# A routed feed-forward kernel on one core: 40 matmuls ahead of the first work, the token list made in one piece, tied gathers, and one transpose for the left-over columns of a routed pair

## The chip, the cores and the metric

One core of a Trainium2 chip runs the whole program. The metric is device time in microseconds (us) of one execution. Engines: PE is the matmul engine (PEld its weight loads), DVE the vector engine, ACT the scalar engine, POOL the general engine, SP the queue that only issues DMAs.

## The reference

4096 tokens (128 batches of 32) with 256 features go through two layers.

```python
# x: (128, 32, 256); subjects and adapters: one of 8 per batch
t = einsum('bct,bcd->bdt', x, w[subjects]) + b[subjects]       # 32x32 mix inside a batch
scores = softmax(t @ gate_w.T); top 2 of 8 experts             # routing
for e in range(8):                                             # routed part, inner size 176
    y += dense_w[:, e] * ((silu(t @ w1[e].T) * (t @ w3[e].T)) @ w2[e].T)
z = (silu(t @ sw1.T) * (t @ sw3.T)) @ sw2.T                    # shared part, inner size 352
x = x + y + z
H = x @ W.T + ((x @ A[adapter].T) @ B[adapter].T) * s          # second layer: linear with adapters
x = x + fp8dot(gelu(fp8dot(H, wg0)) * fp8dot(H, wg1), w_linear)  # hidden size 1024, fp8 operands
```

## The kernel before

The program is written by hand, one instruction stream for each engine, with semaphores between them. The order of the streams is the order of the code; no scheduler moves anything. Tokens are handled in 32 tiles of 128 (`TILES`), four to a group, so 8 groups of 512 tokens (`GROUPS`); `EARLY` is 6.

Products in full precision are made of three matmuls over high and low halves in fp32r (`three`, L1096, L1097 and L1098). ACT writes the high half of an operand (a copy that rounds) and DVE the low half (a subtraction).

The stages, with their time in the profiled execution:

1. **Opening, 0 to 44 us.** For each group: DVE picks the 32x32 matrices of the batches (L659, L660) and spreads them into block-diagonal operands `bd` (L671, semaphore `bd_ready`); PE multiplies (`condition`, L1110); ACT adds the bias (`conditioned`, L448); PE transposes (L1122); ACT keeps the transposed tile (`keep_xT`, L461); PE makes the router's logits (`router`, L1130). SP loads `x` and stores the result `kept`.
2. **Shared part and list, 44 to 128 us.** PE runs `shared_up` and `shared_down` of groups 0 to 5 while DVE sorts out the routing. The slots of the experts are filled by a sum of outer products: `listed` (L1170) multiplies 64 one-hot pairs into bank 5, and DVE turns the sum into the gather indices `perm` (L901). In the same stretch DVE writes the low halves of the routed weights of experts 2 to 7 (`routed_weight_lo`, L752), which `routed_up` waits for (`rw_split`).
3. **Routed part, 128 to 281 us.** 71 slot tiles in 36 pairs (`PAIRS`; the last holds one tile). For a pair POOL gathers the tokens (L387), and PE takes these steps: `routed_T` (transpose of the tokens, L1235), `routed_up` (L1096 to L1098, 352 columns), `routed_hT` (transpose of the hidden values, L1257), `routed_down` (back to 256 columns). The loop runs `routed_T(n + 1)`, `routed_hT(n - 1)`, `routed_up(n)`, `routed_down(n - 1)`. The inner size of 176 is 128 + 48, so a tile's hidden values `hr` are transposed in two blocks; DVE writes the 48 left-over columns twice (at 0 and at 64, L919), so that after the transpose partitions 0 to 47 can hold their high half and 64 to 111 their low half (L930).
4. **Shared part of groups 6 and 7, first gathers, 281 to 317 us.** POOL gathers the two expert results of each token from `slots_out` (`gather_tile`, L394, two DMAs a tile), DVE combines them (L975, L982), and PE starts the second layer for group 0 (`adapters_down`, `linear`, `adapters_up`). DVE clips its result to fp8 (`to_h8`, L1009, waits for `H_done`), which the first fp8 matmul waits for.
5. **Second layer, 317 to 458 us.** For each group `ffn_up` (L1346, 8 steps of 4 matmuls), `ffn_down` (L1365), and between them the next group's linear part. In each group POOL adds the residual of the previous one (`final`, L409) and gathers two groups ahead: `gather(g)` waits for `comb_done` alone, and then issues its 8 DMAs one after the other.

The last group is written out by halves of two tiles: `ffn_down(g, 0)` then `ffn_down(g, 1)`, each followed by a copy on ACT, an addition on DVE and a store on SP.

## Time and profile before

| | us |
|---|---|
| median of 3 runs | 458.88 |
| lowest and highest | 458.27, 459.74 |
| the profiled execution | 459.88 |
| its span, first to last instruction | 458.1 |
| mean granted clock of PE | 0.987 of full |

The span lies 1.78 us under the time of the same execution. "Idle before" of a row is the time in which the engine did nothing ahead of it, and what ended it. PEclk is the granted clock of PE as a share of 2.4 GHz.

### The profile page before, as it was taken

The numbers are of one execution on the slowest core, as the hardware profiler recorded it, in microseconds if no ns is written. First come the engines' busy times: TensorE is split into PE (matmuls) and PEld (weight loads), VectorE is DVE, ScalarE is ACT, GpSimd is POOL, SyncE is SP. The second block draws the span as 40 slices with busy tenths as digits, with TensorE's granted clock in tenths as the row PEclk, the third lists the DMA queues.
The fourth block names the chain that finished last, engine by engine and source line by source line (L and its number), as shares of the span: only waits on it lengthen the run. The fifth ranks groups of instructions, "written<-read, shape, count | busy, mean of one in ns | idle before, by whom it ended". The sixth has DMA issues, their size and how long they took to land.

```text
span 458.1 us, 8166 instructions
## 1 busy us (share of the span) xinstructions
PE 432.9 (95%) x2732; PEld 354.9 (77%) x2732; DVE 309.4 (68%) x701; ACT 249.2 (54%) x514; POOL 181.9 (40%) x188
## 2 busy tenths in 40 slices
PE   4899999999969999999999999995999999999996
PEld 3798788887769999999999997873567557557563
DVE  6972587899774666665666653663967867867844
ACT  2578445658314565555555553432754854855844
POOL 0000506930063444444444401675045756756120
PEclk9999999999998999999999999998899999999999
DMA  7988330000052555545555541332022332322111
GB/s 220 326 286 260 113 110 0 1 0 1 2 156 70 172 155 159 158 150 159 144 174 156 154 102 69 87 99 81 0 72 69 113 92 73 104 90 84 47 46 47
DMA packets 37383, 50.40 MB, mean 110 GB/s; under 512 B 4608, under 2 KB 30592, under 8 KB 37344
## 3 DMA queue, kind: packets, MB, share of 16 engines
q1 hardware_dynamic: 30000, 31.81, 21.1%
q0 software_dynamic: 6480, 17.70, 14.6%
q8 instruction: 24, 0.39, 0.3%
q10 hardware_dynamic: 864, 0.37, 0.3%
q14 instruction: 15, 0.12, 0.1%
HBM read 32.17 MB, written 17.69 MB: 109 GB/s over the span
## 4 chain that ended last, share of the span: by engine, by line
PE 86%; DVE 4%; ACT 3%; issue 2%; another core or an unknown queue 2%; DMA 1%; POOL 1%; SPq 0%; DVEq 0%
PE bank L1096 16%; PE bank L1097 15%; PE bank L1098 15%; PE bank L1346 13%; PE bank L1365 6%; PE bank L1110 4%; PE bank L1257 3%; PE bank L1235 3%; PE bank L1130 3%; PE bank L1273 2%; PE bank L1272 2%; PE bank L1312 2%; PE bank L1122 1%; PE bank L1170 1%
## 5 line engine op out<-in xcount | busy, mean ns | idle before, releaser
L387 POOL DMA_INDIRECT xg<-kept,perm x71 | 67.6, 952 | 102.6 <-PE bank L1235 61.1
L1346 PE MATMUL bank<-h,wg 128*128 128x512 fp8e4 x256 | 64.0, 393 | 4.8 <-DVE h L1009 4.8
L1346 PEld LDWEIGHTS bank<-h,wg 128*128 128x128 fp8e4 x256 | 23.1, 100 | 40.0 <-ACT ff L610 11.8
L928 DVE TENSOR_TENSOR hrl<-bank,hrh 128x256 fp32r<-128x256 f32 (+1 forms) x36 | 15.2, 422 | 54.2 <-ACT hrh L552 52.9
L1096 PE MATMUL bank<-w13h,xgl 128*128 x142 | 49.5, 348 | 0.0
L608 ACT ACTIVATE gel<-bank 128x512 bf16<-128x512 f32 x64 | 40.1, 627 | 12.2 <-PE bank L1346 9.1
L1098 PE MATMUL bank<-w13h,xgh 128*128 x142 | 46.5, 327 | 0.0
L1097 PE MATMUL bank<-w13l,xgh 128*128 x142 | 46.3, 326 | 0.0
L394 POOL DMA_INDIRECT ga<-slots_out,slot x32 | 31.8, 994 | 28.7 <-SPq L347 18.7
L610 ACT ACTIVATE ff<-bank 128x512 bf16<-128x512 f32 x64 | 40.6, 635 | 0.3 <-PE bank L1346 0.3
L394 POOL DMA_INDIRECT gb<-slots_out,slot x32 | 36.8, 1148 | 9.8 <-issue 9.8
L1096 PE MATMUL bank<-xsh,sw13l 128*118 128x512 f32 (+1 forms) x96 | 38.5, 401 | 1.5 <-ACT sil L490 0.8
L559 ACT ACTIVATE yr<-bank 128x512 f32<-128x512 f32 (+1 forms) x36 | 21.3, 592 | 33.9 <-PE bank L1273 33.9
L1021 DVE TENSOR_TENSOR actb<-gel,ff 128x512 bf16<-128x512 bf16 x64 | 27.6, 431 | 17.2 <-ACT ff L610 17.1
L409 POOL TENSOR_TENSOR fin<-xm,ob 128x512 f32<-128x512 f32 x14 | 16.2, 1155 | 55.6 <-ACT ob L616 52.1
L1098 PE MATMUL bank<-xsh,sw13h 128*118 128x512 f32 (+1 forms) x96 | 37.8, 394 | 0.0
L547 ACT ACTIVATE silr<-bank 128x176 f32<-128x176 f32 x71 | 22.8, 321 | 26.1 <-PE bank L1098 23.5
L1365 PE MATMUL bank<-wl,act 128*128 128x256 fp8e4 x256 | 33.1, 273 | 0.4 <-DVE act L1029 0.4
L1365 PEld LDWEIGHTS bank<-wl,act 128*128 128x128 fp8e4 x256 | 23.7, 98 | 10.3 <-issue 3.7
L377 POOL TENSOR_SCALAR places<-cst,placef 128x72 f16<-128x72 f32 x28 | 23.0, 841 | 19.9 <-DVE placef L811 19.9
L1097 PE MATMUL bank<-xtL,sw13h 128*118 128x512 f32 (+1 forms) x72 | 28.3, 393 | 0.0
L616 ACT ACTIVATE ob<-bank 128x512 bf16<-128x512 f32 x16 | 9.6, 597 | 33.6 <-PE bank L1365 33.6
(180 smaller groups left out, 1187.4 us busy)
## 6 DMA issues: line engine op xcount, KB each, us to landing
slots_out<-yr SPq DMA_DIRECT2D x35, 256.0 KB
xres<-in_x SPq DMA_DIRECT2D x7, 512.0 KB, 5.3
kept<-xtr SPq DMA_DIRECT2D x7, 512.0 KB, 3.2
out_x<-fin SPq DMA_DIRECT2D x7, 512.0 KB
w13raw<-in_rw SPq DMA_DIRECT2D x8, 352.0 KB, 3.5
w2raw<-in_rw SPq DMA_DIRECT2D x8, 256.0 KB, 3.7
wgst<-in_wgate SPq DMA_DIRECT2D x16, 128.0 KB
xg<-kept,perm POOLq DMA_INDIRECT x71
```

The source lines that it names most:

```text
L377: pool.tensor_scalar(places[:, c, :], cst[:, C_J:C_J + SLOT_TILES], placef[:, c:c + 1], cst[:, C_TOKEN + t:C_TOKEN + t + 1], ALU.is_equal, ...
L387: pool.indirect_dma_start(out=xg[:, i % 2, j, :], out_offset=None, in_=kept, in_offset=bass.IndirectOffsetOnAxis(perm[:, 2 * i + j:2 * i + ...
L394: pool.indirect_dma_start(out=buf[:, g % 2, j, :], out_offset=None, in_=slots_out, in_offset=bass.IndirectOffsetOnAxis(slot[:, k, g * GT + ...
L547: act.activation(silr[:, j, :], bank[j][:, 0:INNER], ACT.Silu).then_inc(s("silr_ready"), 1)
L608: act.activation(gel[:, b, :], bank[b][:, :], ACT.Gelu_apprx_tanh).then_inc(s("gel_ready"), 1)
L610: act.activation(ff1[:, b, :], bank[2 + b][:, :], ACT.Copy).then_inc(s("ff1_ready"), 1)
L1021: dve.tensor_tensor(actb[:, c % 4, :], gel[:, b, :], ff1[:, b, :], ALU.mult).then_inc(s("act_ready"), 1)
L1096: pe.matmul(dst, al, bh, start=first, stop=False, skip_group_check=True)
L1097: pe.matmul(dst, ah, bl, start=False, stop=False, skip_group_check=True)
L1098: return pe.matmul(dst, ah, bh, start=False, stop=last, skip_group_check=True)
L1346: ins = pe.matmul(bank[bk][:, :], wg8[:, kk, half, c * P:(c + 1) * P], h8[:, k, kk, :], start=(kk == 0), stop=(kk == KC - 1))
L1365: ins = pe.matmul(bank[6 + half][:, (j % 2) * D:(j % 2 + 1) * D], act8[:, c, j * P:(j + 1) * P], wl8[:, c, :], start=(c == 0 and j % 2 == ...
```

## The change

Seven edits are made at once:

- **Warm.** PE issues 40 matmuls of 128 columns on a constant (`onesb`) ahead of `condition(0)`; POOL writes that constant first. SP issues the load of the table ahead of that of the subjects.
- **`keep_xT(0)`** stands ahead of `conditioned(1)` on ACT.
- **List.** All 64 products of `listed` stand ahead of `shared_up(5)` parts 2 to 5, where 32 stood ahead of parts 2 and 3 and 32 behind them. On DVE `perm` stands two steps earlier, and `shared_x_lo(EARLY)` (L682) behind `routed_mul(0)`.
- **Gathers.** `gather(g)` waits ahead of tile j for `gate_done` of step 2j of `ffn(g - 2)`.
- **One transpose.** The left-over columns of both tiles of a pair lie in one block (`hr[:, 2]`, 48 at column 0, 48 at column 64), so that a pair has three transposes, the third into bank 7. ACT copies it with an instruction of its own, broadcast to both tiles; DVE then writes the low half of tile 0 at partitions 64 to 111 and that of tile 1 at 0 to 47, in two instructions. `hr_hi` and `hr_split` count two steps a pair, and `routed_down` waits for the second only ahead of its last four matmuls.
- **Last group.** Tiles 0 and 1 go through bank 6, tile 2 through bank 3, tile 3 through bank 4, each with its own copy, addition and store.

```diff
@@ sync
+            sp.dma_start(tabr[:, :, :].rearrange("p j e -> p (j e)"), table).then_inc(s("table_in"), 16)
             sp.dma_start(subj[:, :], subjects).then_inc(s("subj_in"), 16)
-            sp.dma_start(tabr[:, :, :].rearrange("p j e -> p (j e)"), table).then_inc(s("table_in"), 16)
...
@@ gpsimd
                 pool.wait_ge(s("comb_done"), (g - 1) * GT)
                 for j in range(GT):
+                    pool.wait_ge(s("gate_done"), (g - 2) * HC + 2 * j + 1)
                     gather_tile(g, j)
...
@@ scalar
             conditioned(0)
+            keep_xT(0)
             conditioned(1)
-            keep_xT(0)
...
-                act.activation(hrh[:, 0:n, :, :].rearrange("p a b c -> p (a b c)"), bank[4][:, 0:n * 2 * P], ACT.Copy).then_inc(s("hr_hi"), 1)
+                act.activation(hrh[:, 0:n, 0, :], bank[4][:, 0:n * P].rearrange("p (a b) -> p a b", a=n), ACT.Copy
+                               ).then_inc(s("hr_hi"), 1)
+                act.activation(hrh[:, 0:n, 1, :], bank[7][:, 0:P].unsqueeze(1).broadcast_to([P, n, P]), ACT.Copy
+                               ).then_inc(s("hr_hi"), 1)
...
@@ vector, routed_mul
-                    dve.tensor_tensor(hr[:, j, P:2 * P].rearrange("p (a b) -> p a b", a=2)[:, :, 0:REST],
-                                      silr[:, j, P:INNER].unsqueeze(1).broadcast_to([P, 2, REST]),
-                                      bank[j][:, INNER + P:2 * INNER].unsqueeze(1).broadcast_to([P, 2, REST]),
+                    dve.tensor_tensor(hr[:, 2, j * LO_AT:j * LO_AT + REST], silr[:, j, P:INNER], bank[j][:, INNER + P:2 * INNER],
                                       ALU.mult).then_inc(s("hr_ready"), 1)
...
@@ vector, routed_h_lo
-                dve.tensor_tensor(hrh[low, 0:n, 1, :], of_tile[low, :, 1, :], hrh[low, 0:n, 1, :].bitcast(F32),
-                                  ALU.subtract).then_inc(s("hr_split"), 1)
+                                  hrh[:, 0:n, 0, :].bitcast(F32), ALU.subtract).then_inc(s("hr_split"), 1)
+                dve.wait_ge(s("hr_hi"), 2 * i + 2)
+                spare = slice(LO_AT, LO_AT + REST)
+                for j, own, other in ((0, slice(0, REST), spare), (1, spare, slice(0, REST)))[0:n]:
+                    ins = dve.tensor_tensor(hrh[other, j, 1, :], bank[7][own, 0:P], hrh[own, j, 1, :].bitcast(F32), ALU.subtract)
+                ins.then_inc(s("hr_split"), 1)
...
@@ tensor
+            pe.wait_ge(s("c_prep"), 1)
+            for _ in range(WARM):
+                pe.matmul(bank[3][:, 0:P], onesb[:, :], onesb[:, :], start=True, stop=True)
             condition(0)
...
-            listed(0, ENTRIES // 2)
-            shared_up(EARLY - 1, parts=range(2, 4))
-            listed(ENTRIES // 2, ENTRIES)
-            shared_up(EARLY - 1, parts=range(4, 6))
+            listed()
+            shared_up(EARLY - 1, parts=range(2, 6))
...
                 for j in range(tiles_of(i)):
-                    for c in range(2):
-                        col = (j * 2 + c) * P
-                        ins = pe.transpose(bank[4][:, col:col + P], hr[:, j, c * P:(c + 1) * P], ident)
+                    pe.transpose(bank[4][:, j * P:(j + 1) * P], hr[:, j, :], ident)
+                ins = pe.transpose(bank[7][:, 0:P], hr[:, 2, :], ident)
...
+            def last_down():
+
+                g = GROUPS - 1
+                pe.wait_ge(s("ob_ready"), g * 2)
+                for c in range(HC):
+                    pe.wait_ge(s("act8_ready"), g * HC + c + 1)
+                    for j in range(2):
+                        ins = pe.matmul(bank[6][:, j * D:(j + 1) * D], act8[:, c, j * P:(j + 1) * P], wl8[:, c, :],
+                                        start=(c == 0 and j == 0), stop=(c == HC - 1), skip_group_check=True)
+                ins.then_inc(s("down_done"), 1)
+                for j, _, b in LAST[1:]:
+                    for c in range(HC):
+                        ins = pe.matmul(bank[b][:, 0:D], act8[:, c, j * P:(j + 1) * P], wl8[:, c, :],
+                                        start=(c == 0), stop=(c == HC - 1))
+                    ins.then_inc(s("down_done"), 1)
```

How the instructions move, at three places.

DVE, from the low halves of expert 3's weights to the first routed product. Before:

```order
L752 TENSOR_TENSOR w13l<-w13raw,w13h 128x704 [waits rw_hi]
L752 TENSOR_TENSOR w2l<-w2raw,w2h 128x512
L901 TENSOR_SCALAR perm<-bank 128x72 [waits r_listed]
L733 TENSOR_TENSOR hsf<-sil,bank 116x512 [waits hs_split,u_done,sil_ready]
L752 TENSOR_TENSOR w13l<-w13raw,w13h 128x704 [waits rw_hi]
L752 TENSOR_TENSOR w2l<-w2raw,w2h 128x512
L740 TENSOR_TENSOR hsl<-hsf,hsh 116x512 [waits hh_ready]
L752 TENSOR_TENSOR w13l<-w13raw,w13h 128x704 [waits rw_hi]
L752 TENSOR_TENSOR w2l<-w2raw,w2h 128x512
L682 TENSOR_TENSOR xsh<-xtT,xsh 128x1024 [waits u_done,xs_hi]
L912 TENSOR_TENSOR xgl<-bank,xgh 128x512 [waits xr_hi,hs_split]
L912 TENSOR_TENSOR xgl<-bank,xgh 128x512 [waits xr_hi]
```

And with the change:

```order
L769 TENSOR_TENSOR w13l<-w13raw,w13h 128x704 [waits rw_hi]
L769 TENSOR_TENSOR w2l<-w2raw,w2h 128x512
L914 TENSOR_SCALAR perm<-bank 128x72 [waits r_listed]
L750 TENSOR_TENSOR hsf<-sil,bank 118x512 [waits hs_split,u_done,sil_ready]
L769 TENSOR_TENSOR w13l<-w13raw,w13h 128x704 [waits rw_hi]
L769 TENSOR_TENSOR w2l<-w2raw,w2h 128x512
L757 TENSOR_TENSOR hsl<-hsf,hsh 118x512 [waits hh_ready]
L769 TENSOR_TENSOR w13l<-w13raw,w13h 128x704 [waits rw_hi]
L769 TENSOR_TENSOR w2l<-w2raw,w2h 128x512
L750 TENSOR_TENSOR hsf<-sil,bank 116x512 [waits hs_split,u_done,sil_ready]
L769 TENSOR_TENSOR w13l<-w13raw,w13h 128x704 [waits rw_hi]
L769 TENSOR_TENSOR w2l<-w2raw,w2h 128x512
```

The row that makes `perm` stood behind the third weight pair of this stretch and now stands behind the first; the pieces of hidden values and weights that stood ahead of it now come behind it.

PE, the step between two pairs of the routed loop (tokens' transposes, hidden values' transposes, first product of the next pair). Before:

```order
L1235 MATMUL bank<-cst,xg 128x128 [waits xr_split,xg_in1]
L1235 MATMUL bank<-cst,xg 128x128 x3
L1257 MATMUL bank<-cst,hr 128x128 [waits hr_split,hr_ready]
L1257 MATMUL bank<-cst,hr 128x128 x3
L1096 ISA [waits hr_ready,xr_split]
L1096 MATMUL bank<-w13h,xgl 128x352
```

And with the change:

```order
L1249 MATMUL bank<-cst,xg 128x128 [waits xr_split,xg_in1]
L1249 MATMUL bank<-cst,xg 128x128 x3
L1269 MATMUL bank<-cst,hr 128x128 [waits hr_split,hr_ready]
L1269 MATMUL bank<-cst,hr 128x128
L1270 MATMUL bank<-cst,hr 128x128
L1110 ISA [waits hr_ready,xr_split]
L1110 MATMUL bank<-w13h,xgl 128x352
```

Four transposes of `hr` have become three, and the third has a line of its own.

DVE, the low halves of one routed pair and the next pair's first steps. Before:

```order
L928 TENSOR_TENSOR hrl<-bank,hrh 128x256 [waits hr_hi]
L930 TENSOR_TENSOR hrh<-bank,hrh 48x2x128
L912 TENSOR_TENSOR xgl<-bank,xgh 128x512 [waits xr_hi]
L918 TENSOR_TENSOR hr<-silr,bank 128x128 [waits silr_ready]
L919 TENSOR_TENSOR hr<-silr,bank 128x2x48
```

And with the change, where `hrh` is written by two instructions of 128 columns, behind a wait of their own, for one of 256:

```order
L941 TENSOR_TENSOR hrl<-bank,hrh 128x256 [waits hr_hi]
L946 TENSOR_TENSOR hrh<-bank,hrh 48x128 [waits hr_hi]
L946 TENSOR_TENSOR hrh<-bank,hrh 48x128
L928 TENSOR_TENSOR xgl<-bank,xgh 128x512 [waits xr_hi]
L934 TENSOR_TENSOR hr<-silr,bank 128x128 [waits silr_ready]
L935 TENSOR_TENSOR hr<-silr,bank 128x48
```

The low half of the left-over columns has gone from one row to two, and the products of these columns (`hr`, 48 columns) are half as wide.

## Rows read from the trace of the kernel before

**Rows 1.** The page: busy time, share of the span and instructions by engine.

```profile
PE 432.9 (95%) x2732; PEld 354.9 (77%) x2732; DVE 309.4 (68%) x701; ACT 249.2 (54%) x514; POOL 181.9 (40%) x188
```

**Rows 2.** Window of the routed loop: length, busy by engine, PEclk, DMA share, GB/s.

```profile
138.00:272.00 134.00, 133.81 (x990) 132.65 (x991) 81.75 (x268) 73.80 (x169) 59.13 (x63) 0.99 0.52 148
```

**Rows 3.** The chain, 0 to 60 us: start, us, what.

```profile
1.18 2.81 DMA tabr<-in_table
...
5.97 2.07 PE bank L1110 x4
...
12.23 1.96 PE bank L1110 x8
...
15.05 0.98 ACT xtT L461 x2
...
20.80 1.73 PE bank L1110 x8
```

**Rows 4.** Timeline of DVE, 0 to 46 us: start, us, line, operation [idle before].

```profile
10.22 0.69 DVE L671 TENSOR_TENSOR bd<-wrow,cst 128x512 f32<-128x512 f32 x1
...
16.59 0.69 DVE L671 TENSOR_TENSOR bd<-wrow,cst 128x512 f32<-128x512 f32 x1
```

**Rows 5.** The chain, 100 to 146 us.

```profile
115.72 2.58 PE bank L1170 x32
...
129.88 2.55 DMA xg<-kept,perm
...
134.78 2.53 another core or an unknown queue
```

**Rows 6.** Timeline of PE, 100 to 146 us.

```profile
130.31 0.63 PE L1235 MATMUL bank<-cst,xg 128*128 128x128 f32 x4 [1.62 <-DMA xg<-kept,perm]
...
138.19 0.66 PE L1257 MATMUL bank<-cst,hr 128*128 128x128 f32 x4 [1.02 <-DVE hr L919]
```

**Rows 7.** Timeline of DVE, 100 to 146 us.

```profile
125.24 0.22 DVE L901 TENSOR_SCALAR perm<-bank 128x72 int32<-128x72 f32 x1
...
128.63 0.92 DVE L752 TENSOR_TENSOR w13l<-w13raw,w13h 128x704 fp32r<-128x704 f32 x1
...
130.08 1.21 DVE L682 TENSOR_TENSOR xsh<-xtT,xsh 128x1024 fp32r<-128x1024 f32 x1
```

**Rows 8.** Windows of 1 us behind two idle times of PE; columns as above.

```profile
140.00:141.00 1.00, 1.00 (x5) 1.00 (x5) 0.97 (x2) 0.32 (x1) 0.00 (x0) 0.50 0.41 115
320.00:321.00 1.00, 1.00 (x3) 0.30 (x2) 1.00 (x3) 0.81 (x2) 0.00 (x0) 0.50 0.00 0
```

**Rows 9.** The chain of the whole span, around one routed pair and one group.

```profile
172.00 0.44 PE bank L1257 x4
...
176.00 0.44 PE bank L1257 x4
...
354.93 5.64 PE bank L1346 x24
```

**Rows 10.** Timeline of PE, 268 to 320 us.

```profile
277.71 0.38 PE L1096 MATMUL bank<-w2h,hrl 128*128 x1 [0.76 <-DVE hrh L930]
```

**Rows 11.** Timeline of DVE, the same stretch.

```profile
280.40 0.29 DVE L930 TENSOR_TENSOR hrh<-bank,hrh 48x128 fp32r<-48x128 f32 x1
...
314.07 0.69 DVE L1009 TENSOR_SCALAR h<-bank 128x512 fp8e4<-128x512 f32 x1 [4.35 <-remote]
316.91 0.69 DVE L1009 TENSOR_SCALAR h<-bank 128x512 fp8e4<-128x512 f32 x1 [2.15 <-remote]
```

**Rows 12.** Timeline of POOL, the same stretch.

```profile
284.10 0.94 POOL L394 DMA_INDIRECT ga<-slots_out,slot  x1 [18.70 <-SPq L347]
...
315.85 0.94 POOL L394 DMA_INDIRECT gb<-slots_out,slot  x1 [0.30 <-issue]
```

**Rows 13.** Timeline of all engines, 317 to 336 us.

```profile
317.66 8.11 PE L1346 MATMUL bank<-h,wg 128*128 128x512 fp8e4 x24 [4.76 <-DVE h L1009]
```

**Rows 14.** The chain, 438 us to the end.

```profile
451.69 2.49 PE bank L1365 x20
```

More of the change, by code:

```diff
@@ L43 @@
 L1_PARTS = 4
+WARM = 40
 EARLY = GROUPS - 2
@@ L617, in down_out, with last_out @@
                                ACT.Copy).then_inc(s("ob_ready"), 1)
+            def last_out():
+                g = GROUPS - 1
+                act.wait_ge(s("fin_ready"), g * 2)
+                for n, (j0, j1, b) in enumerate(LAST):
+                    act.wait_ge(s("down_done"), g * 2 + n + 1)
+                    act.activation(ob[:, j0:j1, :].rearrange("p a b -> p (a b)"),
+                                   bank[b][:, 0:(j1 - j0) * D], ACT.Copy).then_inc(s("ob_ready"), 1)
             def ffn(g, first=False, last=False):
@@ L624, in ffn @@
                         x_hi(g + 1)
-                if not last:
-                    xa_hi(g + 1)
+                if last:
+                    last_out()
+                    return
+                xa_hi(g + 1)
                 down_out(g, 0, first)
```

87 lines of the change are left out of this document (40 added, 47 removed).

## The prediction

> **What bounds the kernel now.** I read the page first: PE is busy for 95% of the span [rows 1]. Then I read the table of windows by stage, because an average hides where PE waits: in the routed loop PE and its weight loads are both busy nearly all the time (133.81 and 132.65 of 134 us) and DVE 81.75 of 134 [rows 2]. There only fewer PE instructions help. Then I read the chain and the timelines at the few places where PE is not full. Five are touched by the change: the opening, the step from the list to the routed loop, the loop's drain, the start of the second layer, and the end.
>
> **Opening.** The first multiplications begin at 5.97 us, and four of them take 2.07 us, 517 ns each; later eight of the same form take 1.73 us, 216 ns each [rows 3]. That is the ratio of PE's two clock levels (1.2 and 2.4 GHz), although PEclk shows full speed for these first microseconds, so here I trust the durations. `condition(1)` begins at 12.23, and then PE stands until 16.03, when ACT has finished the copies of `keep_xT(0)` that wait behind `conditioned(1)` (0.98 from 15.05) [rows 3].
>
> With the change, group 0 should run at full clock, if 40 small matmuls are enough to raise it and end in time. Their price is not in the trace. The nearest row is the list's product, 2.58/32 = 81 ns each [rows 5], at half clock 161 ns at most: 40 of them take 6.5 us, and from about 1.0 they end by 7.5. At the lower bound they cost half of that. I take 4 to 5 us, so they are hidden ahead of the 5.97; even at 6.5 they are, for what comes next is a different bound: `condition(1)` needs the second `bd`, which DVE finishes at 10.22 + 0.69 = 10.91 [rows 4]. The table is issued first, which brings DVE's chain forward by up to one issue (the table's 2.81 us begin at 1.18; I take 0.4) [rows 3]. So `condition(1)` begins at about 10.5 instead of 12.23: 1.7. `keep_xT(0)` is then long done, and the wait of about 2 us before `router(0)` disappears: 3.7 to 4.0 in all. The next `bd` that could stop PE is that of group 3, 17.28 less 0.4 = 16.9 [rows 4]; PE asks for it at 20.80 before [rows 3], and at 20.80 - 3.9 = 16.9 now. So DVE catches it just there, and 3.8 remains. Behind it PE is the slower of the two. **Term 1: 3.8**, between 2.0 (the clock rises no earlier, only the copy's wait goes) and 4.2.
>
> **From the list to the routed loop.** The first 32 products end at 118.30 [rows 5], yet `perm` comes at 125.24 [rows 7], since 12 large matmuls, the other 32 products and DVE's own work lie between. With all 64 together the list ends near 120.6 (115.72 and less than twice 2.58), and `perm` is next on DVE: 4.6 earlier. The first gather lands at about 125.7 rather than 130.3, so the first transposes no longer wait 1.62 [rows 6]. What is late next? DVE: the low halves of the weights, which ended at 130.16 (`L682` begins at 130.08 [rows 7]), wait for hidden products that now come later: the first of them needs 12 matmuls of 512 columns behind the list, at least 12 x 213 ns, so about 123.4. From there DVE has four weight pairs, 1.45 each (128.63 to 130.08) [rows 7], and four pieces of hidden values at about 0.6: the last weight ends at 131.6. Then come two `xgl` and two additions of 512 columns, at most 0.69 each [rows 11], and five small operations of about 0.25: `routed_hT(0)` at about 135.6, where it was 138.19 [rows 6], so 2.6 earlier. Part of the old delay is a wait of ACT of 2.53 us that ends with no releaser in the profile [rows 5]; behind these pauses PE runs at a granted 0.50, 1.2 GHz [rows 8], and the 12 matmuls of `routed_up(1)`, 352 columns each, cost 352/1.2 = 293 ns instead of 147, 1.7 in all. If both go, the loop is 2.6 + 1.7 = 4.3 earlier. **Term 2: 3.9**, a little under, as four estimates are in it; if ACT's wait comes back and the clock falls again, 1.0 to 1.5.
>
> **The routed loop.** One pair takes 4.00 us (172.00 to 176.00), and its four transposes of `hr` 0.44, 0.11 each [rows 9]. One of four goes in 35 pairs: 3.85. This is only a gain if nobody else takes PE's place. ACT writes the high half in two instructions; the first needs half the columns, so DVE starts about 0.2 earlier than now. DVE then has two instructions of 48 partitions at 0.29 each [rows 11] where it had one; at worst 0.29 more per pair, while it is busy only 61% [rows 2]. Copy, subtraction and these two make them ready some 1.5 after the transposes, and `routed_down` asks for them behind 12 matmuls of 352 columns and 6 of 256, at least 1.76 + 0.64 later. I count this at nothing; the cover is `routed_up`. In the drain, where no `routed_up` of full length covers it, PE waited 0.76 [rows 10]; the first half of `routed_down` now needs `hrl` alone, which is ready 0.7 earlier. **Term 3: 4.5**, between 3.5 and 4.7.
>
> **The start of the second layer.** PE has no work for 4.76 us and then 24 matmuls take 8.11 us [rows 13], where the same 24 of a later group take 5.64 [rows 9]; the granted clock behind the pause is 0.50, 1.2 GHz [rows 8]. PE waits for two `to_h8` of DVE, and these wait 4.35 and 2.15 us, ended by nothing that the profile knows ("remote") [rows 11]. PE stopped at 312.9, and behind the product that the second conversion needs it still had 12 matmuls of 256 columns (1.3 us), so both operands were there by 311.6: some 3 us of the first wait and all of the second are unexplained. What stands beside them: POOL issues 24 gathers nearly without a break from 284.10, and the last begins at 315.85 [rows 12], the second `to_h8` at 316.91. ACT's unexplained wait [rows 5] also falls into a burst of eight gathers. With the change the eight gathers of group 2 wait for `gate_done`, so they begin only when `ffn_up(0)` runs; the burst is 16 and ends by about 307. If that releases DVE, the two conversions end at 312.3, PE goes on at 312.9 without a pause, keeps its clock (8.11 - 5.64 = 2.47), and loses about 0.7 because DVE still has two additions and four combinations ahead of the first activation. **Term 4: 4.76 + 2.47 - 0.7 = 6.5**, or 0 if the wait stays. In later groups POOL is itself slower than `gate_done`, so nothing else moves.
>
> The Trainium skill (SBUF — State Buffer, "Who interferes with whom") says that a DVE instruction with at most one SBUF input, outside the two-port modes, does not contend with GpSimd. `to_h8` reads PSUM only, so by this rule the port is not the cause and moving the gathers need not help; term 4 would be 0. It is a reason to give the case without term 4 a real chance. The trace shows the coincidence, not the cause.
>
> **End.** The last 20 matmuls end at 451.69 + 2.49 = 454.18 [rows 14], and until the span's end at 458.1 lie 3.9 us of a copy, an addition and a store for two tiles. With one tile each of them handles half as much, but each has a fixed part. If all were fixed it gives 0, if none 2.0; I take **term 5: 0.9**.
>
> **Sum.** 3.8 + 3.9 + 4.5 + 6.5 + 0.9 = 19.6. The profiled execution takes 459.88: 440.3. The median of the runs is 1.0 below it, 439.3. I say 440.0, since the handoffs of 0.02 to 0.14 us that the chain shows at each new dependency are not in the terms.
>
> **Rivals.**
> - *All but term 4* (20 in 100): the conversions wait as before, and PE turns cold again. 439.3 + 6.5 = 445.8. For it: the rule above. Against it: the wait ends with the burst.
> - *Term 4 comes, term 2 does not* (13 in 100): a wait of ACT or of PE for the third gather returns while the clock falls. 439.3 + 2.7 = 442.0, up to 443.5 if term 1 falls to its lower bound.
> - *Neither comes* (12 in 100): 439.3 + 6.5 + 2.7 = 448.5.
> - *The routed loop gets slower* (3 in 100): PE waits in every pair for the second `hr_split` or for ACT's extra instruction. All other terms give 15.1, so the kernel is slower than before once a pair takes 0.43 us more than now; at 0.6 more it is 465. It would take more than 1.1 us over my estimate in the chain behind `hr`. DVE's idle third speaks against it.
> - *The change gives more than the sum* (5 in 100): under 437, if DVE's load at the start of the second layer costs nothing and the handoffs shrink.
>
> **How the numbers follow.** My forecast has the rest, 47 in 100, with its own range from 437.5 to 442. To leave no more than 2 in 10 out, the range goes from 437.0 to 448.0: it takes in the second case, the case without term 4 and a part of the third. Changes under 0.3% (1.4 us) can't be told from none here. Only the slower loop, or several lost terms together, bring the time near 458: faster 0.95, same 0.02, slower 0.03.
>
> **What the profile will show.** Right: the multiplications of `condition(0)` at 216 ns each, `condition(1)` at about 10.5; `perm` about 8 us earlier on the clock of the trace (4.6 and 3.8); a pair of 3.9 us in the chain; no "remote" wait at `to_h8` and 24 matmuls of the first `ffn_up` in under 6.5 us. Wrong: the half clock still there at 140 or 320 less the shift, a pair of 4.0 with a wait for `hrh`, or ACT or DVE waits with no releaser at a new place.

## The result, and the profile after

The changed kernel takes 444.04 us (median of 4 executions, 443.26 to 450.91), the kernel before in the same series 458.57 (453.03 to 459.74). The ratio is 0.9699, with a 95% interval from 0.9618 to 0.978. The time lies in the range that was given and 4 us above the number.

Executions of one and the same kernel fall into two kinds some 7 us apart, with TensorE's mean granted clock above or below 0.98; the profile of the changed kernel shown first (450.91 us, span 449.1, clock 0.973) is of the lower kind, so the profile of a further execution (E1: 443.66 us, span 441.0, clock 0.996) is shown beside it.

The page of the 450.91 us execution, the rows of PE and of PEclk in 40 equal slices of 11.2 us each, and the busy time of PE:

```profile
PE 436.1 (97%) x2737; PEld 360.3 (80%) x2737; DVE 310.1 (69%) x736; ACT 251.1 (56%) x551; POOL 188.7 (42%) x188
...
PE   6999999999997999999999999999999999999996
...
PEclk9998589999979999999999999999999999999999
```

The same two rows in E1, where a slice is 11.0 us:

```profile
PE   7999999999999999999999999999999999999996
...
PEclk9999999999899999999999999999999999999999
```

PE is busy nearly everywhere, as before [rows 1]. What differs most between the two executions is the fourth to sixth slice: in the first PE runs at half clock there. The windows of the first execution show it (columns: window, length, busy by engine, PEclk, DMA share, GB/s):

```profile
144.50:278.50 134.00, 133.79 (x1005) 133.50 (x1004) 86.63 (x313) 79.06 (x212) 59.66 (x63) 1.00 0.54 158
44.00:54.00 10.00, 10.00 (x40) 9.16 (x41) 0.79 (x2) 0.58 (x2) 5.23 (x4) 0.50 0.21 62
...
62.00:80.00 18.00, 18.00 (x110) 15.45 (x109) 14.04 (x30) 9.54 (x15) 4.34 (x5) 1.00 0.26 76
```

The second row has forty matmuls in 10 us at a granted 0.50 (1.2 GHz), with no wait among them; at 62 us the clock is full again. The fall itself stands beside a short wait. It is granted from 41.48 on, and the timeline has this row just there:

```profile
41.27 0.57 PE L1110 MATMUL bank<-xsh,sw13l 128*118 128x512 f32 x1 [0.71 <-DVE xtL L699]
```

The same wait of 0.71 us for the first `xtL` is in E1, at 41.38, and there the clock stays full.

The first row answers to [rows 2]: in 134 us of the routed loop PE now does 1005 instructions where it did 990, and DVE's busy time has gone from 81.75 to 86.63.

**The opening.** The chain of the first execution (start, us, what):

```profile
9.12 1.26 DVE wrow L677
...
10.40 0.70 DVE bd L688
...
11.15 1.99 PE bank L1124 x8
13.14 1.68 PE bank L1144 x16
...
17.53 1.98 PE bank L1124 x8
```

`condition(1)` begins at 11.15 instead of 12.23 and `router(0)` follows it at once, at 13.14, where it waited for the copies until 16.03 [rows 3]. `condition(3)` begins at 17.53, where it was 20.80. The second group's `bd` starts at 10.40, 0.2 later than in [rows 4], not 0.4 earlier: DVE now waits for the subjects at 3.67, where it waited for the table at 4.01.

**The list.** The timeline of PE in E1 (start, us, engine, line, operation, tiles, shape, count, and in brackets the idle time before it and what ended it):

```profile
112.64 3.27 PE L1187 MATMUL bank<-places,lanes_first 128*128 128x72 f16 x36
116.00 3.83 PE L1187 MATMUL bank<-places,lanes_rest 128*128 128x72 f16 x28
119.64 0.76 PE L1110 MATMUL bank<-xsh,sw13l 128*118 128x512 f32 x1
120.19 0.63 PE L1111 MATMUL bank<-xtL,sw13h 128*118 128x512 f32 x1
...
135.83 0.66 PE L1249 MATMUL bank<-cst,xg 128*128 128x128 f32 x4 [0.82 <-DMA xg<-kept,perm]
136.32 0.38 PE L1269 MATMUL bank<-cst,hr 128*128 128x128 f32 x2
```

The 64 products take 7.0 us, not under 5.2 [rows 5]. The large matmuls behind them last 0.63 instead of 0.39 and start 0.43 apart instead of 0.23; the profile grants 0.50 from 118.57 to 121.98. `routed_hT(0)` comes at 136.32.

Why 7.0? The mean of a row hides two rates. These are windows of E1 (columns as above):

```profile
112.00:114.00 2.00, 2.00 (x30) 1.75 (x28) 0.83 (x2) 1.55 (x3) 0.00 (x0) 1.00 0.00 0
114.00:116.00 2.00, 1.92 (x15) 1.36 (x15) 1.90 (x4) 0.63 (x1) 0.00 (x0) 1.00 0.00 0
...
118.00:120.00 2.00, 2.00 (x15) 1.55 (x15) 0.13 (x1) 0.00 (x0) 0.00 (x0) 0.64 0.00 0
```

From 114 us on PE does 15 or 16 in each 2 us, at full clock as well as at half. By their starts in the trace, the first 16 products come 33 ns apart and the others 126 ns apart, with a few longer steps, up to the last one; nothing changes in this when the clock falls at 118.57. The kernel before has the same two rates: in its first row of 32 the first 16 start 33 ns apart and the rest 125. So the 81 ns of [rows 5] are no price of a product, but the mean of a fast head and a slow rest, and a row of 64 has only one head.

**One routed pair** in the chain of the first execution, to be held against [rows 9]:

```profile
171.39 0.44 PE bank L1249 x4
171.83 0.22 PE bank L1269 x2
...
175.25 0.44 PE bank L1249 x4
175.69 0.22 PE bank L1269 x2
```

A pair takes 3.86 us where it took 4.00. In the drain the wait of 0.76 [rows 10] has become one of 0.2.

**The start of the second layer**, timelines of DVE, of POOL and of PE of the first execution:

```profile
309.72 1.37 DVE L1025 TENSOR_SCALAR h<-bank 128x512 fp8e4<-128x512 f32 x2 [1.32 <-PE bank L1112]
```

```profile
304.56 0.95 POOL L396 DMA_INDIRECT gb<-slots_out,slot  x1 [0.30 <-issue]
312.94 1.14 POOL L396 DMA_INDIRECT ga<-slots_out,slot  x1 [7.43 <-PE bank L1361]
```

```profile
311.58 3.80 PE L1361 MATMUL bank<-h,wg 128*128 128x512 fp8e4 x16
315.61 2.02 PE L1361 MATMUL bank<-h,wg 128*128 128x512 fp8e4 x8 [0.23 <-ACT ff L616]
```

The gathers of the third group wait 7.43 us as written. The two `to_h8` run back to back without the waits of [rows 11], and 24 matmuls end 6.05 us after the first began, where it was 8.11 [rows 13]. Seen alone, this looks like term 4 come true.

### The profile page after: what moved, and what is told of

It is laid out like the page before. It is cut to its first block, busy times and chain, and to the rows that moved or that the text cites. A ratio compares the mean times of both kernels' runs of the same rounds, so it can differ in the third digit from the quotient of the medians.

```text
span 449.1 us, 8254 instructions
## 1 busy us (share of the span) xinstructions
PE 436.1 (97%) x2737; PEld 360.3 (80%) x2737; DVE 310.1 (69%) x736; ACT 251.1 (56%) x551; POOL 188.7 (42%) x188
## 4 chain that ended last, share of the span: by engine, by line
PE 90%; DVE 4%; ACT 2%; DMA 1%; POOL 1%; issue 1%; SPq 0%; DVEq 0%; ACTq 0%
PE bank L1110 18%; PE bank L1112 17%; PE bank L1111 17%; PE bank L1361 12%; PE bank L1376 5%; PE bank L1249 3%; PE bank L1144 3%; PE bank L1124 3%; PE bank L1288 2%; PE bank L1287 2%; PE bank L1269 2%; PE bank L1327 2%; PE bank L1187 2%; PE bank L1136 1%; DMA xg<-kept,perm 1%; PE bank L1270 1%
## 5 line engine op out<-in xcount | busy, mean ns | idle before, releaser
L389 POOL DMA_INDIRECT xg<-kept,perm x71 | 69.3, 976 | 95.2 <-PE bank L1249 58.6
L1361 PE MATMUL bank<-h,wg 128*128 128x512 fp8e4 x256 | 61.6, 380 | 0.2 <-ACT ff L616 0.2
L1110 PE MATMUL bank<-xsh,sw13l 128*118 128x512 f32 (+1 forms) x96 | 41.4, 431 | 1.0 <-DVE xtL L699 0.7
L396 POOL DMA_INDIRECT gb<-slots_out,slot x32 | 38.1, 1191 | 9.8 <-issue 9.8
L1112 PE MATMUL bank<-xsh,sw13h 128*118 128x512 f32 (+1 forms) x96 | 40.4, 421 | 0.0
L379 POOL TENSOR_SCALAR places<-cst,placef 128x72 f16<-128x72 f32 x28 | 25.6, 935 | 26.4 <-DVE placef L828 26.4
L1111 PE MATMUL bank<-xtL,sw13h 128*118 128x512 f32 (+1 forms) x72 | 31.0, 430 | 0.0
L1376 PE MATMUL bank<-wl,act 128*128 128x256 fp8e4 x224 | 29.2, 273 | 0.0
L1376 PEld LDWEIGHTS bank<-wl,act 128*128 128x128 fp8e4 x224 | 20.8, 98 | 8.8 <-issue 3.7
L497 ACT ACTIVATE hsh<-hsf 118x512 fp32r<-118x512 f32 (+1 forms) x18 | 11.4, 632 | 29.2 <-DVE hsf L750 27.0
```

The source lines that it names most:

```text
L379: pool.tensor_scalar(places[:, c, :], cst[:, C_J:C_J + SLOT_TILES], placef[:, c:c + 1], cst[:, C_TOKEN + t:C_TOKEN + t + 1], ALU.is_equal, ...
L389: pool.indirect_dma_start(out=xg[:, i % 2, j, :], out_offset=None, in_=kept, in_offset=bass.IndirectOffsetOnAxis(perm[:, 2 * i + j:2 * i + ...
L396: pool.indirect_dma_start(out=buf[:, g % 2, j, :], out_offset=None, in_=slots_out, in_offset=bass.IndirectOffsetOnAxis(slot[:, k, g * GT + ...
L1110: pe.matmul(dst, al, bh, start=first, stop=False, skip_group_check=True)
L1111: pe.matmul(dst, ah, bl, start=False, stop=False, skip_group_check=True)
L1112: return pe.matmul(dst, ah, bh, start=False, stop=last, skip_group_check=True)
```

## The experiments

All twelve were compared with the kernel before on the same chip. The text uses three numbers of each: the median of all its executions, the median of those with a mean granted clock of 0.98 or more, and how many lie under 0.98. For the kernel before the three are 453.46, 451.98, 5 of 13 on the chip of E1 to E4; 457.81, 453.70, 5 of 7 on that of E5 to E8; 453.08, 452.00, 8 of 30 on that of E9 to E12.

**E1, the changed kernel again.** No edit.

> The changed kernel once more, unaltered, for an execution of the common kind: the profiled one took 450.9 where three others took 443.3 to 444.8. Theory A: the 7.6 us are the stretch at half clock from 41 to 56 us of that profile, so a profile at 443 shows PEclk full there, condition(1) still near 11.1, perm near 116.5, and the second layer 7 us earlier. Theory B: part of the 7.6 lies in the gather of 2.76 us and its slow transfer (PE waited 2.02 at 142 to 144), and is gone too. In both a pair takes 3.86 and the first ffn_up has no wait without a releaser.

Measured: 445.52 (443.63 to 447.61, 4 executions), none under 0.98; ratio 0.9799, interval 0.9678 to 0.992. The span is 8.1 us shorter than in the first profile. `perm` comes at 119.87 instead of 126.02, so 6.15 of the 8.1 were already there at the list, that is, in the stretch of half clock from 42 to 58 us. The gather of 2.76 us is in both profiles alike; PE waited 0.82 for it here and 2.02 in the first. Theory A holds for 6 of the 8 us and B for 1.2; the rest is the half clock behind the list, longer in the first profile (about 124 to 130 us) than here (119 to 122). Theory A's 116.5 for `perm` was too early: the list takes its 7.0 us in both.

**E2, the spaced gathers alone.**

```
             def gather(g):
                 pool.wait_ge(s("comb_done"), (g - 1) * GT)
                 for j in range(GT):
+                    pool.wait_ge(s("gate_done"), (g - 2) * HC + 2 * j + 1)
                     gather_tile(g, j)
```

> The kernel before with the wait in gather alone. Theory A (the burst of 24 gathers holds back to_h8): about 6.5 us less, 452 us, no wait of DVE without a releaser at 310 to 320, and no half clock there. Theory B (the wait of to_h8 comes by chance or from another source, such as instruction fetches): no difference within 0.3%, 458, and the wait of 4 us is still in the profile or missing from both kernels in the same share of runs.

Measured: 452.87 (450.12 to 460.33, 10 executions), median 452.64 of those at 0.98 and above, 2 of 10 under it; ratio 1.0002, interval 0.9976 to 1.0028. Theory B: no difference. That the time is near theory A's 452 says nothing, since both theories were reckoned from 458.6, and the kernel before itself took 453.46 on this chip.

**E3, the one transpose alone**, with everything that belongs to it on ACT, DVE and PE. The core of the edit:

```
                 for j in range(tiles_of(i)):
-                    for c in range(2):
-                        col = (j * 2 + c) * P
-                        ins = pe.transpose(bank[4][:, col:col + P], hr[:, j, c * P:(c + 1) * P], ident)
+                    pe.transpose(bank[4][:, j * P:(j + 1) * P], hr[:, j, :], ident)
+                ins = pe.transpose(bank[7][:, 0:P], hr[:, 2, :], ident)
                 ins.then_inc(s("hr_T"), 1)
```

> The kernel before with the routed pair's left-over columns through one transpose alone. Theory A (every pair 0.14 shorter as the changed kernel's profile shows, 4.00 to 3.86, and the drain 0.5 shorter): 35 x 0.14 + 0.5 = 5.4 less, 453 us. Theory B (some of it is given back before the second layer, where POOL and DVE are asked earlier): 3 or less, 455.5 and more.

Measured: 446.96 (444.18 to 452.44, 4 executions), 446.35 at 0.98 and above, 1 of 4 under it; ratio 0.9778, interval 0.963 to 0.9926. Against 451.98 that is 5.6 less, where theory A had 5.4. The profile says more. POOL issues all 24 gathers nearly without a break here (four gaps of 0.57 to 1.11 us), as the kernel before does, and still DVE's conversions start with no wait of the unexplained kind (POOL first, then DVE, timelines of E3):

```profile
278.88 0.94 POOL L394 DMA_INDIRECT ga<-slots_out,slot  x1 [17.36 <-SPq L347]
...
310.65 0.95 POOL L394 DMA_INDIRECT gb<-slots_out,slot  x1 [0.30 <-issue]
```

```profile
305.60 1.37 DVE L1010 TENSOR_SCALAR h<-bank 128x512 fp8e4<-128x512 f32 x2 [1.32 <-PE bank L1099]
```

The two conversions lie inside the burst. E4's profile shows the same: 24 gathers from 279.96 to 310.72, and a wait of 1.32 us for PE at 305.66.

**E4, the opening alone.** The edits, of which E9 and E10 each keep a part:

```
+            sp.dma_start(tabr[:, :, :].rearrange("p j e -> p (j e)"), table).then_inc(s("table_in"), 16)
             sp.dma_start(subj[:, :], subjects).then_inc(s("subj_in"), 16)
...
             conditioned(0)
+            keep_xT(0)
             conditioned(1)
-            keep_xT(0)
...
+            pe.wait_ge(s("c_prep"), 1)
+            for _ in range(WARM):
+                pe.matmul(bank[3][:, 0:P], onesb[:, :], onesb[:, :], start=True, stop=True)
             condition(0)
```

> The kernel before with the opening alone: 40 small matmuls, the table first, keep_xT(0) ahead of conditioned(1). Theory A: the 3.8 us of the opening reach the end, 454.8 us. Theory B: the earlier warm TensorE brings a stretch at half clock between 40 and 56 us (as in the changed kernel's profile) in part of the runs: then 454.8 in most and 7 more, 462, in some. Theory C: the wait for the loaded weights or for POOL's list eats the gain: 458.

Measured: 447.72 (447.16 to 454.48, 4 executions); the one at 454.48 has a clock of 0.980, the other three 0.995 or more. Ratio 0.9827, interval 0.9683 to 0.9971. Against 451.98 it is 4.3 less, where theory A had 3.8 (its 454.8 is reckoned from 458.6), and one execution in four is of the kind that theory B feared.

**E5, the list alone**, with `perm` and `shared_x_lo(EARLY)` on DVE moved as in the change. On PE:

```
-            listed(0, ENTRIES // 2)
-            shared_up(EARLY - 1, parts=range(2, 4))
-            listed(ENTRIES // 2, ENTRIES)
-            shared_up(EARLY - 1, parts=range(4, 6))
+            listed()
+            shared_up(EARLY - 1, parts=range(2, 6))
```

> The kernel before with the 64 list products together, perm two steps earlier and shared_x_lo(EARLY) behind routed_mul(0), nothing else. Theory A (64 small products in a row bring TensorE's clock down, as in the second profile of the changed kernel: the last 32 at 134 instead of 81 ns and then 5 large matmuls at half clock; DVE stands for 6 us and its work arrives late): routed_hT(0) about 2 us later than in the kernel before without ACT's unexplained wait, and 2 us slower in executions without a stall, about 453.8 against 451.8. Theory B (my term 2): 3.9 faster at that place, 448.

Measured: 460.87 (453.66 to 461.41, 4 executions), 3 of 4 under 0.98; the verdict against 457.81 is open. The three lie 2.7 us above the median of the five like ones of before (460.95 against 458.2), and the one at 0.991 lies inside before's own (453.01 and 454.39). The profile is plainer. In it PE runs the list thus:

```profile
122.95 3.31 PE L1171 MATMUL bank<-places,lanes_first 128*128 128x72 f16 x36
126.19 3.83 PE L1171 MATMUL bank<-places,lanes_rest 128*128 128x72 f16 x28
...
130.38 0.63 PE L1098 MATMUL bank<-xtL,sw13h 128*118 128x512 f32 x1
```

The same 3.83 and 0.63 as in E1, now without any of the other edits. Theory A has the loss and the half clock right. Its "134 instead of 81 ns" is the misreading named above: here too the first 16 products start 33 ns apart and the rest 126, from 123.4 on, while the clock falls only at 127.41.

**E6, the changed kernel with the list's part undone** (the diff of E5 the other way, with `perm` and `shared_x_lo(EARLY)` where they were).

> The changed kernel with the list's part undone, all else kept. Theory A: 2.2 us faster than the changed kernel's 443.65, 441.4 in most runs, no half clock at 116 to 122. Theory B (term 2 gains): slower than it by 1 to 4, 444.7 to 447.5.

Measured: 441.46 (440.38 to 442.74, 4 executions), none under 0.98 and three of four at 1.000; ratio to before 0.9677, interval 0.9596 to 0.9759. Five of the seven executions of before that the ratio is taken against lie under 0.98; under the median of the other two (453.70) it is by 12.2. It is 2.2 less than the changed kernel's two executions at 0.996 on another chip (443.65), 4.1 less than the median of its four, and 4.4 less than E8 on the same one, which has the whole list and lacks only the spaced gathers. Its PE timeline:

```profile
112.59 2.73 PE L1186 MATMUL bank<-places,lanes_first 128*128 128x72 f16 x32
117.99 0.30 PE L1186 MATMUL bank<-places,lanes_first 128*128 128x72 f16 x4
118.13 1.91 PE L1186 MATMUL bank<-places,lanes_rest 128*128 128x72 f16 x28
127.29 0.63 PE L1251 MATMUL bank<-cst,xg 128*128 128x128 f32 x4 [1.66 <-DMA xg<-kept,perm]
...
133.99 0.38 PE L1271 MATMUL bank<-cst,hr 128*128 128x128 f32 x2
```

And in windows of `listed` alone (PE's busy time and count, then PEclk):

```profile
118.50:119.00 0.50, 0.48 (x15) 1.00 0.00 0
119.00:120.00 1.00, 1.00 (x8) 1.00 0.00 0
```

The second row of 32 has a fast head of its own, of 24 products, and 8 slow ones behind it, 126 ns apart as in E1. Some 23 more of the steps between products are of 33 instead of 126 ns than in E1, which makes the 2.2 us. `routed_hT(0)` is at 133.99, 2.3 earlier than in E1, though `perm` comes 2.4 later (122.3). Theory A.

**E7, the list in two halves, `perm` one step earlier.** E6 with these edits:

```
             hidden_mul(5, 1)
             routed_weight_lo(4)
+            dve.wait_ge(s("r_listed"), 1)
+            dve.tensor_scalar(perm[:, :], bank[5][:, 0:SLOT_TILES], float(MIDDLE), None, ALU.add).then_inc(s("r_perm"), 1)
             hidden_lo(5, 1)
             routed_weight_lo(5)
-            dve.wait_ge(s("r_listed"), 1)
-            dve.tensor_scalar(perm[:, :], bank[5][:, 0:SLOT_TILES], float(MIDDLE), None, ALU.add).then_inc(s("r_perm"), 1)
...
-            shared_x_lo(EARLY)
...
             routed_mul(0)
+            shared_x_lo(EARLY)
```

> The changed kernel with TensorE's order of the kernel before (32 products, 12 matmuls, 32 products) and perm on DVE one step earlier than before, after routed_weight_lo(4); shared_x_lo(EARLY) stays behind routed_mul(0). If the list gains by coming earlier without costing TensorE its clock: perm 1.7 earlier than in the kernel with the list undone, the 1.6 us wait of the first transposes for their gather gone, 440 us. If the third gather's landing then bounds the start of the loop: no more than 441.4.

Measured: 440.25 (438.46 to 442.37, 4 executions), none under 0.98; ratio to before 0.9647, interval 0.9558 to 0.9736, against the same executions of before as in E6. `perm` stands at 120.23, 2.1 earlier than in E6, and the wait of the first transposes is gone. What is late next:

```profile
129.08 0.66 PE L1252 MATMUL bank<-cst,xg 128*128 128x128 f32 x4 [1.59 <-DMA xg<-kept,perm]
...
133.23 0.44 PE L1272 MATMUL bank<-cst,hr 128*128 128x128 f32 x2 [1.13 <-DVE hr L935]
```

`routed_hT(0)` is 0.8 earlier than in E6: the second gather's landing takes back half of the gain. The two medians differ by 1.2 us, with ranges that overlap, so E7 is the fastest version by its median and not shown to beat E6.

**E8, the changed kernel without the spaced gathers.** The line of E2 taken out.

> The changed kernel without the wait in gather. Theory A (the burst is not what stopped DVE; two profiles with the whole burst show no such wait): 443.6 as with the wait, and the same share of slow executions. Theory B (the burst stops DVE in part of the executions): some runs 6 us longer, 450, with a wait without a releaser at to_h8.

Measured: 445.81 (443.76 to 447.19, 4 executions), none under 0.98. The changed kernel itself has 445.52 in E1. Theory A, as far as four executions tell; no conversion waits without a releaser in its profile.

**E9, the warm-up alone**: E4 without the moved `keep_xT(0)`.

> The kernel before with the 40 small matmuls, onesb first on POOL and the table's transfer first; keep_xT(0) stays behind conditioned(1). Theory A (the opening needs both: warming ends condition(0) 2 us sooner, but router(0) then still waits for the two copies): some 1 us faster than before in executions without a half-clock stretch at 45 to 62, 450. Theory B (warming alone carries term 1): as fast as the whole opening, 447.5. On the long half-clock stretch (20 of 38 and fewer executions without the opening, 2 of 25 with it): if TensorE's early activity keeps it away, at most 1 of 6 here has a mean clock under 0.98; if not, 2 to 4.

Measured: 456.75 (451.14 to 461.08, 12 executions), 453.56 at 0.98 and above, 6 of 12 under it; ratio 1.0038, interval 0.9993 to 1.0082. Warming alone gives nothing, less than theory A's 1 us. Its windows show one reason (PEclk is the third column from the right):

```profile
4.00:8.00 4.00, 2.24 (x18) 1.64 (x15) 3.76 (x7) 1.00 (x2) 0.00 (x0) 1.00 0.84 247
8.00:12.00 4.00, 3.75 (x13) 2.89 (x14) 3.93 (x5) 1.66 (x4) 0.00 (x0) 0.57 0.86 293
```

PE has warmed up and then waits 1.71 us for the input tile, and from 8.1 us it is granted half clock again. In E1 it waited 0.83 in the same place and kept its clock. The other reason is the one that theory A names: `router(0)` still waits 1.99 us for the copies, and the clock falls once more at 18.35.

**E10, the moved copy alone.**

```
             conditioned(0)
+            keep_xT(0)
             conditioned(1)
-            keep_xT(0)
```

> The kernel before with keep_xT(0) ahead of conditioned(1) alone. Theory A (only the 2 us wait at router(0) goes, the cold start stays): 1.5 to 2 us faster than before in like executions, 449.5 to 450. Theory B (the copy was hidden by the next bd anyway): no change. The long half-clock stretch: 2 to 4 of 6 executions under 0.98 as before, if it is warming that keeps it away.

Measured: 447.78 (447.50 to 449.72, 7 executions), all at 0.994 and above; ratio 0.9922, interval 0.9895 to 0.9949. This is the whole of E4's time, with two lines moved. The timeline of PE:

```profile
6.36 3.89 PE L1110 MATMUL bank<-xres,bd 128*128 128x256 f32 x8 [6.36 <-DVE bd L671]
10.04 2.01 PE L1122 MATMUL bank<-cst,xtr 128*128 128x128 f32 x8
11.89 1.89 PE L1110 MATMUL bank<-xres,bd 128*128 128x256 f32 x8
13.62 1.85 PE L1130 MATMUL bank<-gatew,xtT 128*128 128x8 f32 x16
```

`condition(0)` is as cold as before (3.89 for 8), yet `condition(1)` begins at 11.89, 0.6 behind E1's 11.26, and `router(0)` follows without a wait. Theory A is right in that the pause goes, but the time is 4.2 under the 452.00 of before, not 1.5 to 2, and the share under 0.98 is not 2 to 4 of 6 but 0 of 7. The first `xtL` starts 2.6 earlier. The rest fits what the profiles show behind the pause, under term 1 below.

**E11, the end alone.**

```
+LAST = ((0, 2, 6), (2, 3, 7), (3, 4, 5))
...
+                for j, _, b in LAST[1:]:
+                    for c in range(HC):
+                        ins = pe.matmul(bank[b][:, 0:D], act8[:, c, j * P:(j + 1) * P], wl8[:, c, :],
+                                        start=(c == 0), stop=(c == HC - 1))
+                    ins.then_inc(s("down_done"), 1)
```

> The kernel before with the last group's output in pieces of two, one and one tile. Theory A (term 5): 0.9 us less from the last matmul to the end of the span, 0.9 in like executions. Theory B (the stores' fixed part is all of it): nothing.

Measured: 453.15 (449.67 to 459.76, 12 executions), 451.59 at 0.98 and above against before's 452.00, 5 of 12 under it; ratio 1.0045, interval 0.9995 to 1.0094. In times it can't be told from nothing. In profiles it can: from the last transpose of `hr` to the end of the span lie 447.9 - 276.8 = 171.1 us here, and 171.8 in E4 and E10 (445.8 - 274.0, 446.1 - 274.3), where the end is as before. That is 0.7. (The change has tile 2 in bank 7 and tile 3 in bank 5, not in banks 3 and 4 as the text on the change says.)

**E12, the changed kernel without the opening** (the edits of E4 the other way).

> The changed kernel without the opening's part. Theory A (the opening gives 2.9 us at the first shared products and keeps the long half-clock stretch away): 446.5 in like executions, and 2 to 4 of 6 with a mean clock under 0.98 and 7 us more, 453. Theory B (the opening has only its own 2.9 us): 446.5, with no more than one slow execution of 6.

Measured: 449.20 (446.65 to 455.68, 12 executions), 448.38 at 0.98 and above, 5 of 12 under it. The share fits theory A; the time is 1.9 over the 446.5 of both theories.

## Why the prediction was right, and where only its number was

The time fell into the range, and three of five terms came near their size. Two had the wrong cause or sign, and a cause that stood in no term made up for them. For each term the profiles are cut at three marks: the start of the first `xtL` of the shared expert, the first and the last transposes of `hr`, and the end of the span. The second and third marks are the first and last start in one line of the view by tile (here E11, whose middle is that of the kernel before, and E6):

```profile
L1267 PE MATMUL bank<-cst,hr x142: 270/273/275, 137.6 to 276.8; 128*128 128x128 f32 x142
```

```profile
L1271 PE MATMUL bank<-cst,hr x71: 271/273/274, 134.0 to 267.6; 128*128 128x128 f32 x71
```

**Term 1, the opening: 3.8 forecast, 2.9 to 4.1 measured.** The first `xtL` starts at 42.91 before, at 40.01 in E1 and at 40.28 in E10. Of 2.9 us the moved copy alone brings 2.6 and the warm-up with the table 0.3. The forecast had given the earlier start of `condition(1)` 1.7 and the copy about 2. The step "from about 1.0 they end by 7.5" was right and did not matter: with PE warm, DVE sets `condition(1)`, and its chain did not come forward by 0.4 but went back by 0.2, since the first thing it needs is `subj`.

What the forecast did not have is a fall of the clock behind the 2 us pause. Of the seven profiles with the old order of the copy, five (E2, E3, E5, E9, E12) have PE at a granted 0.50 from 17 or 18 us on, for 3.4 us, and their first `xtL` starts at 43.6 to 44.1 instead of 42.9. Of the seven with the moved copy none has it. Against those five the opening is worth 3.6 to 4.1.

**Term 2, the list: a gain of 3.9 forecast, a loss of 2.3 measured** (136.3 in E1 against 134.0 in E6, everything else equal). The step that failed is "with all 64 together the list ends near 120.6 (115.72 and less than twice 2.58)". On the clock of E1 that is 117.5; it ended at 119.6. I took the duration of 32 such products for half of that of 64. But 16 of the 32 are a fast head, and one row of 64 has one head: 15 steps of 33 ns and 48 of 126 are 6.5 us, which the trace of before could have told.

In all fourteen profiles the first head is of 16 products and the slow step is 125 or 126 ns, at full clock and at half. The reason for it is in part argued: each product has a wait instruction of its own on PE, and in E1 the 28 of the first line (L1183) start 126 ns apart too, from 1.5 us before the first product on. So PE's queue seems to need 126 ns a product, and those that it has passed while PE was at larger work start 33 ns apart. No run left the waits out.

All five profiles with the whole list in one piece (the changed kernel's, E1, E5, E8, E12) have a stretch of half clock that begins in its slow part, from 3 to 7 us long; none of the other nine has one there. The products cost 2.2 more (7.0 against 2.73 and 2.05 in E6), which is the missing second head, and the large ones behind about 1 (five at 0.43 for 0.23), which is the clock. The rest is DVE's: it stands from 117.6 to 123.8 with only `perm` in between, since the hidden products that it waits for are behind the list, and then has all the weight halves to do, the last ending at 131.9, where the forecast has 131.6 - 3.8 = 127.8. The gather was on time, and nobody could use it.

**Term 3, the loop: 4.5 forecast, about 5.5 measured.** The first to the last transpose of `hr` takes 139.2 in E11 (139.7 in E10, 139.9 in E4), 133.9 in E1 and 133.6 in E6. The mechanism was right, the pair's share is 0.14 instead of 0.11: three transposes take 0.33 where four took 0.44, and 0.02 to 0.03 go from the stretches beside them. As forecast, no engine took PE's place: the two halves of `hr_split` are never waited for in the loop.

**Term 4, the start of the second layer: 6.5 forecast, nothing measured.** From the last `hr` transpose to the end lie 458.1 - 279.1 = 179.0 in the profile of before, 171.8 in E4 and E10, which have the same code there. So the waits of [rows 11] and the cold stretch behind them cost 7.2 us, a good estimate of the 6.5 and 0.7; but they are in that one profile and in none of the other thirteen, whether the burst is there or not (E3, E4: whole; E2: spaced and equal in time). The step that failed is "the trace shows the coincidence": I wrote this down, and still gave its being a cause more than 6 in 10. The rule of the Trainium skill (SBUF — State Buffer, "Who interferes with whom") that stood against it was right here: `to_h8` with its PSUM input lies inside E3's burst at its usual 691 ns. What ended the wait in that one execution stays open. The other two waits with no releaser are in the same profile alone, the 2.56 us of ACT ahead of `silr` (the 2.53 of [rows 5]) and 1.4 us of DVE ahead of `xres`: the execution that I read everything from was an unusual one.

**Term 5, the end: 0.9 forecast, 0.7 measured** (E11), too little for times alone. Over all profiles the stretch is 170.7 to 171.1 us in the seven with the new end and 171.7 to 172.1 in the six with the old one beside that of before, so it may be 1.0.

**The sum in like executions** is 2.9 - 2.3 + 5.5 + 0.7 = 6.8. On E1's chip the medians of those at 0.994 and above are 451.82 and 443.65, 8.2 apart. Before has four executions at 1.000 on another chip, 449.6 in the median, and the changed kernel has none, since the list always costs it some clock; against these it is 6.0. The 6.8 lies between. It has term 1 without the short fall at 17 us; with it, it is up to 8.0. The medians of the first series differ by 14.5. The rest is no term of mine. It is the stretch of half clock from about 42 us on, which costs 6 us (E1: `perm` at 126.02 with it, 119.87 without), or the wait of [rows 11]. The three executions of before at 458.3 to 459.7 lie where on the other chips those under 0.98 lie (457.5 to 460.4), and where the profiled one with that wait lies (459.88); which they had isn't known. The fourth, 453.03, is too short for either. And the change itself makes this stretch rare. Of the executions with `keep_xT(0)` ahead of `conditioned(1)` (the changed kernel, E1, E4, E6, E7, E8, E10) 2 of 32 have a mean clock of 0.98 or less; of those without (before, E2, E3, E5, E9, E11, E12) 40 of 104. On one chip, in one series, it is 0 of 7 (E10) against 24 of 66. E9 has the warm-up and not the moved copy: 6 of 12. So it goes with the copy and not with the 40 matmuls; the 0 of 7 by itself could be chance (at a share of 24 in 66 it comes about once in 24 times), the 2 of 32 hardly. All that the copy changes for PE is that the 2 us pause at 14 to 16 us is gone. The profiles show a step between. Six of the fourteen have half clock from 41 to 46 us on, three for 17 us (the changed kernel's, E5, E9) and three for 3.4 us (E2, E3, E8), and in all six it begins within 0.35 us of the end of the 0.71 us wait for the first `xtL`. All fourteen have that wait. Of the five with the short fall at 17 us four are among the six, of the nine without it two. Why the same wait costs the clock in one execution and not in the next isn't shown.

Of the rivals "neither comes" (448.5) describes the terms best, and "all but term 4" (445.8) and the forecast (440.0) missed in opposite directions what the median then averaged out. That the number was within 1% is luck in part: a gain of 6.5 that was no gain, and 7 us of a kind that I had not seen in a single profile.

## What to carry to other kernels

A wait in one profile is one observation. Before a term is built on it, look at the spread of the times and of the granted clocks of several executions: a term as large as the distance between two groups of executions may be that distance. A row of small products, each with a wait of its own, has two prices here, 33 ns for a head of 16 to 24 products and 126 ns for the rest, so a half taken from the trace isn't half of the whole: look at the starts, or at counts in short windows, before a mean is used as a price. And an earlier result gains nothing when the move that makes it earlier starves the engine that sets the next step: here DVE's work was the bound, and the list had been put in front of what DVE was waiting for.

## What the runs showed of the hardware

- Of 64 products of 72 columns in one row, each behind a wait instruction, the first 16 start 33 ns apart and the others 126 (E1). This is so at a granted 1.00 and at 0.50. Split by 12 large matmuls, the second part has a fast head of its own, of 24 (E6).
- In the five profiles with the 64 in one piece the clock falls to 0.50 in the slow part, for 3.4 or 6.8 us. With two rows of 32 it does not, in nine profiles.
- A stretch of half clock can begin beside a wait of only 0.71 us and last for 17 us with PE fully busy, in one execution and not in the next of the same program (the changed kernel's first profile and E1). A mean clock of 0.98 or less is in 40 of 104 executions with a 2 us pause of PE some 26 us earlier, and in 2 of 32 without it.
- Behind a pause of 2 us at 14 to 16 us the clock falls to 0.50 for 3.4 us in five of seven profiles.
- 40 small matmuls ahead of the first real one bring full speed to it (4 in 1.10 us in E6, where they took 2.07) only when the operands are there soon enough. After 1.71, 1.93 and 2.20 us of waiting for the input PE is at half clock again (E9, E4, E8), after 0.83 to 1.13 it is not (E1, E6, E7); but once it kept its clock over 1.68 us (the changed kernel's first profile), so the wait alone doesn't decide it.
- In all profiles with the list in one piece and in no other, one gather on POOL, the fifth, takes some 2.7 us instead of 0.95. Ahead of it POOL has stood idle, from 125.3 to 130.0 in E1. Here it is in E1:

```profile
129.97 2.76 POOL xg L389
132.73 0.30 issue
133.03 2.75 DMA xg<-kept,perm
```

  It costs PE 0.8 us there. Why it takes so long isn't in the profile, and it wasn't tried apart: another gather that starts after 7.43 us of idle time takes 1.14 (the start of the second layer above).
